# Turning gathered embedding rows with transposing DMAs instead of TensorE transposes, in a fused DLRM tower

## The reference: what is computed

```python
e = stack([tbl_f[ids[:, f]] for f in range(32)], axis=1)   # [2048, 32, 64]: one row of 64 per field
z = e.sum(-1)                                              # [2048, 32]
# for each of the 496 pairs i < j of fields, a 64 x 64 kernel K[p]:
outer[b, p] = e[b, i, :] @ K[p] @ e[b, j, :]
h = concat([z, outer, dense_ctx], axis=1)                  # 32 + 496 + 16 = 544 columns
h = relu(h @ W_top1 + b_top1)                              # 512
h = relu(h @ W_top2 + b_top2)                              # 256
y = h @ W_top3                                             # [2048, 1]
```

## Time and profile before

| | |
|---|---|
| Median of 3 runs | 1235.91 us |
| The profiled execution's own time | 1238.17 us |
| Its span, first to last instruction | 1236.4 us |
| Mean granted TensorE clock | 0.945 of 2.4 GHz |
| PE busy | 1074.5 us (87%) |
| DVE busy | 628.0 us (51%) |
| POOL busy | 483.8 us (39%) |
| ACT busy | 142.5 us (12%) |
| DMA | 29.24 MB, 16384 of 24376 packets from the gathers |

### The profile page before, as it was taken

The page is one execution under the profiler, slowest core; times in us unless marked ns, Lnnn a source line. Parts: engine busy times, 40 slices in busy tenths (PEclk is TensorE's granted clock), DMA queues, the critical chain, the costliest instruction groups (busy, mean ns, idle before and its releaser), DMA issues.

```text
span 1236.4 us, 30329 instructions
## 1 busy us (share of the span) xinstructions
PE 1074.5 (87%) x13964; PEld 460.2 (37%) x13964; DVE 628.0 (51%) x658; ACT 142.5 (12%) x219; POOL 483.8 (39%) x518
## 2 busy tenths in 40 slices
PE   1565737898989888999999999989998999999998
PEld 0453614343334233334343443333343343333333
DVE  0331412264546353656665654556664655589880
ACT  0100110101001101201010021210020020210101
POOL 7444373325543443454445433354445423400000
PEclk9877768899989789999999999999999999999999
DMA  9100010001010000010010000000011000000000
GB/s 335 38 17 18 16 26 13 15 11 21 19 22 12 16 17 14 15 21 18 17 20 20 18 13 13 15 19 19 19 19 20 19 10 15 16 3 2 3 3 0
DMA packets 24376, 29.24 MB, mean 24 GB/s; under 512 B 13366, under 2 KB 13624, under 8 KB 24123
## 3 DMA queue, kind: packets, MB, share of 16 engines
q0 software_dynamic: 16384, 16.81, 7.0%
q1 hardware_dynamic: 7856, 10.49, 2.5%
q10 hardware_dynamic: 10, 0.01, 0.0%
HBM read 27.27 MB, written 0.01 MB: 22 GB/s over the span
## 4 chain that ended last, share of the span: by engine, by line
PE 85%; issue 11%; DVE 1%; another core or an unknown queue 1%; DMA 1%; POOL 1%; ACT 0%; DVEq 0%; ACTq 0%; POOLq 0%
PE y L631 48%; PE accs L649 25%; PE y L611 3%; PE y L710 2%; PE y L693 2%; PE y L681 2%; DVE prod L576 1%; PE y L686 1%; PE y L723 1%; POOL rows L384 1%; DMA rows<-tbl,ids_sb 0%; ACT xt L430 0%; PE y L662 0%; DMA ids_sb<-ids 0%
## 5 line engine op out<-in xcount | busy, mean ns | idle before, releaser
L576 DVE TENSOR_TENSOR prod<-y,xt 128x1024 f32<-128x1024 f32 (+3 forms) x570 | 587.5, 1080 | 561.9 <-PE y L631 373.3
L384 POOL DMA_INDIRECT rows<-tbl,ids_sb x512 | 483.1, 944 | 597.3 <-DVE prod L576 309.2
L631 PE MATMUL y<-xt,kw 64*32 64x512 f32 (+2 forms) x8432 | 647.8, 560 | 66.9 <-issue 53.0
L649 PE MATMUL accs<-prod,ones_strip 64*32 64x512 f32 (+2 forms) x4960 | 352.5, 526 | 67.5 <-issue 66.6
L631 PEld LDWEIGHTS y<-xt,kw 64*32 64x32 f32 (+1 forms) x8432 | 236.8, 115 | 422.5 <-issue 384.4
L649 PEld LDWEIGHTS accs<-prod,ones_strip 64*32 64x32 f32 x4960 | 149.0, 112 | 232.2 <-issue 208.2
L430 ACT COPY xt<-y 128x1024 f32<-128x1024 f32 (+2 forms) x48 | 34.9, 728 | 608.0 <-PE y L611 513.0
L611 PE MATMUL y<-ident,rows 128*128 128x128 f32 x256 | 42.3, 289 | 21.4 <-DMA rows<-tbl,ids_sb 16.2
L548 DVE TENSOR_REDUCE z_rows<-rows 128x8 f32<-128x512 f32 (+2 forms) x80 | 42.9, 570 | 15.2 <-DMA rows<-tbl,ids_sb 15.2
L611 PEld LDWEIGHTS y<-ident,rows 128*128 128x128 f32 x256 | 28.7, 142 | 49.8 <-issue 42.7
L461 ACT COPY h_in<-accs 128x1024 f32<-128x1024 f32 (+2 forms) x10 | 8.4, 842 | 221.1 <-PE accs L649 141.4
(11 more groups left out here) (22 smaller groups left out, 67.5 us busy)
## 6 DMA issues: line engine op xcount, KB each, us to landing
rows<-tbl,ids_sb POOLq DMA_INDIRECT x512
kw<-pair_k SPq DMA_DIRECT2D x14, 512.0 KB
w_sb<-w SPq DMA_DIRECT2D x1, 1024.0 KB
w_sb<-w SPq DMA_DIRECT2D x1, 512.0 KB
kw<-pair_k SPq DMA_DIRECT2D x1, 384.0 KB
kw<-pair_k SPq DMA_DIRECT2D x1, 256.0 KB, 4.1
w1z_sb<-w1z SPq DMA_DIRECT2D x1, 256.0 KB
ids_sb<-ids SPq DMA_DIRECT2D x1, 240.0 KB, 2.7
```

What stands on the lines that cost most here:

```text
L384: pool.indirect_dma_start(out=rows[:, s, c, h, :], out_offset=None, in_=tables[f], in_offset=bass.IndirectOffsetOnAxis(ap=ids_sb[:, b, f:f ...
L576: nc.vector.tensor_tensor(prod_part(t, d, n), y_part(t, d, n), x, ALU.mult).then_inc(y_read, n)
L631: last = nc.tensor.matmul(y[columns, h, :], kw[part, d, columns], xt[part, slot_of(t, units[h][0] // 2), 0:w], start=True, stop=True)
L649: last = nc.tensor.matmul(accs[32 * q:32 * q + 32, n, 0:w], ones_strip[part, STRIPS - 1 - s:2 * STRIPS - 1 - s], prod_part(t, u // 2)[part ...
```

## The change

- **Rows are turned by DMA from tile 1 on.** The 240 transposes of tiles 1 to 4 on PE go; tile 0 keeps its 16. ACT copies a couple's gathered rows into `split`, the low and the high 16 bits of each float apart (`split_rows`). SP issues one transposing DMA for the couple (2 x 3 or 2 x 4 blocks of 128x128 of 16 bits; 192 or 256 KB) from `split` into `halves`, each after the one before has landed. ACT copies the halves together into `xt` (`join_halves`). Both buffers have two slots. 64 splits, 64 DMAs and 64 joins; the 32 copies of PE's transposes from PSUM in tiles 1 to 4 go. Steps wait for `joined`.
- **Their order.** A join stands three steps (of width 512) before the first use of its couple, joins at least 2.5 such steps apart, a split 5 before its join. GATHER_LEAD is 48 in place of 56 and counts from the split; a slot of `rows` is free once its couple is split. `xt` has 18 slots in place of 20. The dense features are loaded from ACT's queue, `z_rows` has two slots, the fields' transpose moves from step 76 to step 108.
- **The field part of the first MLP layer first, in the steps' shape.** It is written as eight products of 64 rows by 32 columns, ahead of the pairs' part.
- **The table of pair kernels piece by piece.** SP issues a piece only when the one before has landed (from the seventh on the one before that).

```diff
+JOIN_MARGIN = 3
+JOIN_SPACING = 2.5
+JOIN_LEAD = 5
...
+def join_at(t, k):
+
+    if t == 1 and k < len(FIRST_JOINS):
+        return full_steps(*FIRST_JOINS[k])
+    d = first_step_of_couple(k) if k < COUPLES - 1 else step_at("inner", SETS - 1, 0) - 6
+    at = full_steps(t, d) - JOIN_MARGIN
+    return at if k == COUPLES - 1 else min(at, join_at(t, k + 1) - JOIN_SPACING)
...
-    goal = FULL_STEPS[STEPS_BEFORE[what]] - GATHER_LEAD + i + 2 * rowsets(t) * (k - what[2])
+    goal = split_at(t, k) - GATHER_LEAD + i
...
+                if c >= 1:
+
+                    sp.wait_ge(k_loaded[c - (1 if c < K_ALONE else 2)], 16)
                 sp.dma_start(kw[:, first:first + n, :],
...
+                    sp.wait_ge(rows_split, i + 1)
+                    if i >= 1:
+
+                        sp.wait_ge(transposed, 16 * i)
+                    if i >= HALF_SLOTS:
+
+                        sp.wait_ge(joined, i - HALF_SLOTS + 1)
+                    sp.dma_start_transpose(halves[:, slot, 0:r, :],
+                                           split[:, slot, 0:r, :].rearrange("p c d -> p (c d)")
+                                           ).then_inc(transposed, 16)
...
+            def split_rows(t, k):
+                n, i, r = couple(t, k), move_number(t, k), 2 * rowsets(t)
+                words = rows[:, n % GATHER_SLOTS, 0:rowsets(t), :, :].rearrange("p c h d -> p (c h d)").bitcast(u16)
+
+                act.wait_ge(gathered[n % GATHER_SLOTS], rows_in(n))
+                if i >= HALF_SLOTS:
+
+                    act.wait_ge(transposed, 16 * (i - HALF_SLOTS + 1))
+                nc.scalar.copy(split[:, i % HALF_SLOTS, 0:r, :].rearrange("p (s c) d -> p s (c d)", s=2),
+                               words.rearrange("p (n s) -> p s n", s=2)).then_inc(rows_split, 1)
+
+            def join_halves(t, k):
+                n, i, r, w = couple(t, k), move_number(t, k), 2 * rowsets(t), WIDTHS[t]
+
+                act.wait_ge(transposed, 16 * (i + 1))
...
+                nc.scalar.copy(xt[:, slot_of(t, k), 0:w].bitcast(u16).rearrange("p (n s) -> p s n", s=2),
+                               halves[:, i % HALF_SLOTS, 0:r, :].rearrange("p (s c) d -> p s (c d)", s=2)
+                               ).then_inc(joined, 1)
...
-            def transpose_couples(t, k, count):
...
-                        last = nc.tensor.transpose(y[:, h, P * c:P * c + P],
-                                                   rows[:, s, c, :, :].rearrange("p h d -> p (h d)"), ident[:])
...
+                    pe.wait_ge(joined, move_number(t, k) + 1)
...
+                for first in range(0, P, 32):
+                    columns = slice(first, first + 32)
+                    for h in range(2):
+                        part = slice(DIM * h, DIM * h + DIM)
+                        j = 2 * pair + h
+                        nc.tensor.matmul(y[columns, h, 0:w], w1z_sb[part, j * P + first:j * P + first + 32],
+                                         z_in[part, 0:w], start=True, stop=False)
+
+                pe.wait_ge(acc_read, CHUNKS * (t + 1) - 1)
```

More of the change, by code:

```diff
@@ L161, in first_tile_work @@
         work[d // p * p].append(("extra", 0, s))
-    for k, d in visits_ahead(1):
-        work[d].append(("couples", 1, k))
     work[108].append(("fields", 0, 0))
@@ L170, in later_tile_work @@
     work = {d: [] for d in range(N_STEPS)}
[L171 removed]
     for d, what in zip(mlp_steps(t), (("mlp1", t - 1, 0), ("mlp1", t - 1, 1), ("mlp2", t - 1, 0), ("mlp3", t - 1, 0))):
         work[d].append(what)
[L174 to L179 removed]
+    work[108].append(("fields", t, 0))
     work[0].append(("extra", t, 0))
[L181 to L182 removed]
+    for n in range(1, SETS):
+        joined = int((join_at(t, 4 * n + 3) - full_steps(t, 0)) * TILE / WIDTHS[t])
+        work[max(step_at("inner", n - 1, 2) + 10, joined + 1)].append(("extra", t, n))
     return work
@@ L188, in plan @@
     work = first_tile_work() if t == 0 else later_tile_work(t)
+    moves = moves_of(t)
     order = []
     for d in range(N_STEPS):
-        order += work[d]
+        order += work[d] + moves[d]
         order.append(("step", t, d))
@@ L205 @@
 PLAN = [what for t in range(TILES) for what in plan(t)]
-Y_ORDER = [what for what in PLAN if what[0] not in ("sum", "extra") and (what[0] != "step" or what[2] % pack(what[1]) == 0)]
+Y_ORDER = [what for what in PLAN if what[0] in ("couple", "fields", "mlp1", "mlp2", "mlp3")
+           or what[0] == "step" and what[2] % pack(what[1]) == 0]
 Y_USES = {what: u for u, what in enumerate(Y_ORDER)}
@@ L326, in tower_program @@
         fields_doubled = sem("fields_doubled")
-        dense_loaded = sem("dense_loaded")
+        dense_loaded = [sem(f"dense_loaded{i}") for i in range(2)]
+        rows_split = sem("rows_split")
+        transposed = sem("transposed")
+        joined = sem("joined")
         small_loaded = sem("small_loaded")
@@ L418, in _, with load_dense @@
+            sp.wait_ge(transposed, 16 * COUPLES * (TILES - 1))
         @block.scalar
         def _(act):
-            def copy_couples(t, k, count):
-                u = copy_use(t, k)
-                w = WIDTHS[t]
-                act.wait_ge(y_full, u + 1)
-                if couple(t, k) >= XT_SLOTS:
-                    before, kb = divmod(couple(t, k) + count - 1 - XT_SLOTS, COUPLES)
+            def load_dense(t):
+                for half in range(2):
+                    act.dma_start(z_rows[:, t % 2, 0:rowsets(t), half, FIELDS:FIELDS + DENSE],
+                                  dense[:, first_block(t):first_block(t) + rowsets(t), :]
+                                  ).then_inc(dense_loaded[t % 2], 16)
@@ L509, in read_mlp3 @@
                               ).then_inc(out_stored, 16)
+            act.wait_ge(z_rows_zeroed, 1)
+            for t in range(2):
+                load_dense(t)
             for what, t, n in PLAN:
                 if what == "couple":
-                    copy_couples(t, n, 1)
-                elif what == "couples":
-                    copy_couples(t, n, 2)
+                    copy_couple(n)
+                elif what == "split":
+                    split_rows(t, n)
+                elif what == "join":
+                    join_halves(t, n)
                 elif what == "extra":
@@ L579, in _ @@
             for what, t, n in PLAN:
-                if what == "couple":
+                if what in ("couple", "split"):
                     field_sums(t, n)
-                elif what == "couples":
-                    for k in range(n, n + 2):
-                        field_sums(t, k)
                 elif what == "step" and n in runs[t]:
@@ L681, in mlp1 @@
                             nc.tensor.matmul(y[:, h, 0:w], w1_sb[:, c, n, j * P:(j + 1) * P], h_in[:, c, n, 0:w],
-                                             start=c == 0 and n == 0, stop=False)
-                for h in range(2):
-                    part = slice(DIM * h, DIM * h + DIM)
-                    j = 2 * pair + h
-                    nc.tensor.matmul(y[:, h, 0:w], w1z_sb[part, j * P:(j + 1) * P], z_in[part, 0:w],
-                                     start=False, stop=False)
+                                             start=False, stop=False)
                 pe.wait_ge(acc_read, CHUNKS * (t + 1))
```

135 lines of the change are left out of this document (71 added, 64 removed).

## The result

Measured: 1277.57 us (median of 4 runs, 1277.35 to 1278.88) against 1235.86 for the kernel before (4 runs, 1235.64 to 1238.09). The ratio is 1.033, 95% interval 1.0315 to 1.0349. The forecast was 1217 us and faster; it is slower, and outside the range. The profiled execution took 1277.42 us, its span is 1275.6. One execution further down, of the table-at-once kernel, took 2853 us where its others took 810 to 814, and is left out of its median.

The account below looks back on a forecast made before the run. PE was taken as the bound: its 32-column work, gather windows, and 128-column work outside them. Terms -14 - 10 + 0 + 5 = -19; 1238.2 - 19 - 2.3 = 1217 us, range 1166 to 1262.

Parts of the forecast that it names:

- windows: Stretches beside bursts of gathers in which PE's 32-column matmuls run at a sixth of their pace.
- Gathers come in other bursts: Tiles 1 to 4 and end of tile 0: same 512 gathers, released differently; estimated +8 us, taken as 0.
- formula 1.25 n - 2.1: Estimated us of PE time that a burst of n gathers costs: 2.9 for 4, 7.9 for 8, 28 for 24.
- rival D: Bunched gathers eat the gain: +18 us, PE's clock drops behind 15-us windows, visits worth only 5; about 1238 us; chance 0.15.
- B: Rival: transposing DMAs open windows like gathers, 64 of 4 us each, half outside present windows: +107, 1325 us; chance 0.11.
- The transposes leave PE: Tiles 1 to 4: removing 240 transposes saves 14 us, since only 11 to 14 visits stand outside windows; bounds 0 and -36.
- The table piece by piece: At the start: DVE's 16.0 us and ACT's 17.6 us stops should go, saving 10 us; 0 if they have another cause.
- The field part: First MLP layer: 32-column products now come where gathers still land, +7 us, less 2 in the clear: +5.
- ACT and the chain of the 64 DMAs hidden: Split, DMA and join chain beside PE: stays hidden up to about 8 us each, estimated about 3 us per DMA; 0.
- Do transposing DMAs slow the matmuls: PE's step matmuls: landing in SBUF alone does not slow them, judged by one 32 KB load; 0 us.
- C: Rival: the DMAs take over 10 us each, joins come late and PE waits at tile starts: 1260 to 1370 us; chance 0.08.
- A: Rival: gather windows shrink too or never were the gathers' doing, so the full 33 us of transposes come off: 1174; chance 0.14.

Follow-up runs that it names:

- table-at-once kernel: The changed kernel with the table of pair kernels sent at once again, as before the change: 812.4 us on chip C, ratio 0.969 to the kernel before.
- batched kernel: The kernel before with the 16 gathers of each visit of tiles 2 to 4 released together: 1426.6 us on chip B, ratio 1.171.
- paced kernel: The changed kernel with gathers released one by one, evenly over a tile's steps, from tile 2 on: 1150.5 us on chip B, ratio 0.944 to the kernel before.
- spaced kernel: The paced kernel with a GpSimd memset behind each gather of tiles 2 to 4: 1136.5 us on chip B, ratio 0.931 to the kernel before.

## Why the prediction was wrong, by its own steps

The tiles without windows (chip D) and with them (chip A) split each tile's time. For the kernel before I use the run with idle transposing DMAs, 0.1% too long. The prediction's 196 us for tile 3 without windows is borne out: 196.4. That a stretch without gathers takes the same on both supports the subtraction: the group in the clear is 5.15 us in the changed kernel on D and on A.

| tile | before, D | now, D | held up, before (A - D) | held up, now (A - D) |
|---|---|---|---|---|
| 0 | 64.4 | 71.7 | 107.1 | 102.7 |
| 1 | 144.4 | 141.5 | 122.5 | 116.5 |
| 2 | 191.1 | 182.1 | 79.1 | 108.7 |
| 3 | 196.4 | 187.9 | 78.0 | 110.3 |
| 4 | 190.7 | 185.0 | 11.8 | 21.6 |
| sum | 787.0 | 768.2 | 398.5 | 459.8 |

The change takes 18.8 us off the work, and the first step is 2.9 us earlier; what is held up grows by 61.3. Together +39.6, of a measured span difference of 39.2.

*Gathers come in other bursts: 0, bounds -13 and +18.* This is the step that failed: what is held up grew by 61 us. It was mis-sized and not missed: the lots of 15, 10 and 10 were seen, and the prediction has +9 for tile 2 and for tile 3. Measured are +30 and +32 (and -6, +10 and -4 in tiles 1, 4 and 0, where -13, +5 and -2 were expected).

First, "in a window of 15 steps also release the next gathers more slowly, which splits the bursts" was the reason to take 0 in place of +8. In the changed kernel the goals come from split positions 2 to 3 full steps apart for couples 0 to 4, with 8 gathers each, so when PE slows down the releases are already overdue, and little splits the run: in tile 3, 15 gathers 1.25 us apart from 883.0 on, one at 906.2, 14 more from 908.0 on, then, when the slots of couples 0 and 1 come free, 16 from 994.2 on.

Second, the lots were taken from the plan, and the trace has others. In the kernel before, the plan's groups of four ran as 4, then 3 and 1. By the formula 1.25 n - 2.1 the plan's bursts of tile 3 give 97 us before and 106 now. The runs of the trace give 79 and 100 (86 and 100 when gathers up to 1.6 us apart count as one run), and 78 and 110 were held up. So counting the real runs makes +14 to +21 out of +9.

The remaining 11 to 18 us of the +32 the formula doesn't give. It is good for long runs (143 us for the batched kernel's tile 3, 148 measured) and too low for short ones: 57 for the paced kernel's tile 3, where 70 were held up on chip B.

One reason for the rest may be that some windows before lay on the visits, which don't mind them, and now lie on steps; the kernel before with even gathers could have shown it, and ran only on D. Another is the clock: 0.94 over 298 us is 36 us at the half level, at the end of and behind the long runs. Most of that time PE has little to do but wait; behind the first run 64 matmuls of steps and sums take 4.00 us (905 to 909, clock 0.73). How these two share the rest is not shown.

Three slips in the working change little: with a sixth taken off throughout, as the prediction says, the formula would be 1.04 n - 1.4, which is 24 us and not 28 for 24 gathers, and +5 in place of the plan's +9; in rival D, 1217 + 18 + 9 is 1244 and not 1238; B's 1325 is 1324.

*The transposes leave PE: -14, bounds 0 and -36.* On D, where nothing hides them, tiles 1 to 4 get 26.1 us shorter, 8.5 to 9 for a full tile but the last. Tile 0 gets 7.3 longer there, which the table in pieces explains (64.3 us with it at once, chip C). On A this part can't be read apart from the windows.

*The table piece by piece: -10.* Wrong. The 16-us stop became two. Rows of the changed kernel's start, DVE, and then the stretch behind the stops:

```profile
25.43 1.29 DVE L648 TENSOR_TENSOR prod<-y,xt 128x512 f32<-128x512 f32 x2 [10.50 <-remote]
...
39.60 1.29 DVE L648 TENSOR_TENSOR prod<-y,xt 128x512 f32<-128x512 f32 x2 [12.69 <-remote]
```

```profile
42.00:44.00 2.00, 2.00 (x22) 2.00 (x22) 0.99 (x4) 0.00 (x0) 1.70 (x2) 1.00 0.81 242
```

The stops together are longer (23.2 us), and they end before the loads do: at 42 to 44 us PE and DVE work beside 242 GB/s. On chip B there are stops either way, 18.9 us in the paced kernel and 12.7 + 7.7 with the table at once. On chip D the kernel before has none while its loads come in (DVE, then all engines from 20 to 25 us):

```profile
19.80 1.29 DVE L591 TENSOR_TENSOR prod<-y,xt 128x512 f32<-128x512 f32 x2 [2.34 <-PE y L646]
...
23.13 1.29 DVE L591 TENSOR_TENSOR prod<-y,xt 128x512 f32<-128x512 f32 x2 [1.85 <-PE y L646]
```

```profile
20.00:25.00 5.00, 4.55 (x32) 3.81 (x34) 2.76 (x6) 2.52 (x8) 3.78 (x5) 1.00 1.03 387
```

So the stops, like the windows, are seen on A and B alone, and what makes them stays open. Tile 1 begins at 189.5 us in both kernels of the result, so even the 2.9 us by which the first step came earlier are gone by then.

*The field part: +5.* 0 within 3 us. *ACT and the chain of the 64 DMAs hidden: 0.* Right: a DMA lets its join go 3.1 us after its issue, and PE waited 11 us in all for joins. The Trainium skill (DMA: Bandwidth & Descriptors, section "Latency and other measured facts") led to an estimate of 3 us; the trace agrees. *Do transposing DMAs slow the matmuls: 0.* Right on C and D, where 64 cost 1 us. On A the rates at the head of a run are the same with one under way (23 and 15 matmuls in 1.25 us) as without (23 and 15). Behind the third gather they are 5 against 8, behind the fourth 3 against 4.5, from 7 and 4 cases with one; from the seventh on 1.4 against 1.6. These are too few to tell, and whether a transposing DMA makes a window of gathers worse is open.

The rivals: D had the mechanism (bunching and the clock behind windows of 15 us), at +18 where the runs gave +61. B didn't happen at its size: with all 64 DMAs the paced kernel is at 0.944 of before. C didn't happen. A's premise, that the windows are not the gathers' doing, is half true: on C and D there are none. The rule of the Trainium skill (SBUF — State Buffer, section "SBUF: two separate sides") that engine and DMA ports can't contend fits chip D, where 134 matmuls begin in ten microseconds beside nine gathers, and not chip A, where 23 do. What differs between the chips no run here shows.

By its own signs: the steps' pace at the third gather, ACT at 249 us, the long slow stretch in the second half of tiles 2 and 3 and the groups at 5.15 came as said. Tile 1 got shorter by 9 and not 10 to 20, "tiles 2 and 3 as long as before to within 5 us" failed, and so did "no idle of 16 us on DVE": two idles of 10.5 and 12.7 came.

## What to carry to other kernels

When a cost depends on how close events follow each other, a schedule's goals have to be followed through its own feedback: compare how many events a step releases with how many it can absorb, over the stretch where goals stand closest, and ask whether they wait for progress or are overdue. A change that gives a queue new release points needs its pacing designed anew (here one rule, 107 us on one chip), also where the amount of work is the same. And an effect that one profile shows without a cause ("the trace doesn't show what makes it") may belong to the chip it was taken on; what is built on it should be tried on a second.

## What the runs showed of the hardware

- The same program takes 1236 us (chip A) and 1218 (chip B, maybe the same chip), and 838 on two others (C, D). Nearly all of it lies where indirect DMAs are under way: of the 399 us between A and D, tile 4, with 32 of the 512 gathers, has 12. In ten microseconds beside nine gathers 134 matmuls of 32 columns begin on D, 23 on A, and 10 further on in that run.
- Where they are held up, it gets worse along a run of gathers 1.25 us apart: 23, 17, 7, 4, 3, then 2 or 1 matmuls in 1.25 us. A gather costs 0.50 us of PE in groups of up to five, 1.44 us apart (spaced kernel, tile 3: 252.5 - 187.9 = 65 us for 128), 0.55 in runs of one to five, 1.25 us apart (paced kernel: 257.6 - 187.9 = 70) and 1.16 in runs of 16 (batched kernel: 344.4 - 196.4 = 148). The times are of chip B, what is taken off of chip D.
- While 10.5 MB of loads come in at the start, DVE and ACT stop for 16 and 17.6 us on chip A, and not at all on D at 387 GB/s.
- The granted clock falls to 0.5 (1.2 GHz) in the second half of a run of 15 gathers, when few matmuls begin (10 in the ten microseconds from 894), and is at 0.73 from 905 to 909, when 64 begin again.
- A transposing DMA of 256 KB from SBUF to SBUF lets the copy that waits for it start 3.1 us after its issue, beside gathers (889.91 to 892.98) and without (1174.40 to 1177.47), and 64 of them beside a busy PE cost 1 us on chips without windows.
